# The second cross attention's chains: three batches five steps apart in place of two in step

## What is computed

```python
c_t = attn_mean @ V                                   # selection result, projected by Wv
x   = layernorm(x_text, g_norm_in, b_norm_in)         # x_text is layernorm(x) of the model
scale_in, shift_in = split(c_t @ W_film_in + b_film_in)
x   = x * (1 + mod_gate * scale_in) + mod_gate * shift_in
y   = s4d(x)                                          # a long convolution, by FFT, plus x * D_skip
scale_out, shift_out = split(c_t @ W_film_out + b_film_out)
y   = y * (1 + mod_gate * scale_out) + mod_gate * shift_out
xt  = x_text + y
h   = gelu(layernorm(xt, g_ffn, b_ffn) @ W1 + b1) @ W2 + b2
out = layernorm(xt + h, g_norm_out, b_norm_out)       # added to x
```

## Time and profile before

| what | value |
|---|---|
| median of 3 runs | 2420.95 us (2419.89 to 2425.65) |
| the profiled execution | 2421.84 us, of which the span is 2420.0 us |
| TensorE busy | 1858.7 us (77% of the span) |
| VectorE busy | 1291.5 us (53%) |
| ScalarE busy | 1060.2 us (44%) |
| GpSimd busy | 790.4 us (33%) |
| mean granted TensorE clock | 0.845 |

### The profile page before, as it was taken

The page is one execution under the profiler, slowest core; times in us unless marked ns, Lnnn a source line. Parts: engine busy times, 40 slices in busy tenths (PEclk is TensorE's granted clock), DMA queues, the critical chain, the costliest instruction groups (busy, mean ns, idle before and its releaser), DMA issues.

```text
span 2420.0 us, 34900 instructions
## 1 busy us (share of the span) xinstructions
PE 1858.7 (77%) x13676; PEld 1137.1 (47%) x13676; DVE 1291.5 (53%) x3082; ACT 1060.2 (44%) x1404; POOL 790.4 (33%) x686
## 2 busy tenths in 40 slices
PE   5789999999999988977466677876876477667752
PEld 2444544554454455655463244544544355455531
DVE  5143232323323016364884869979789754535557
ACT  1367567657657842212342435455455201005440
POOL 6144333335414100000320357857777021210001
PEclk7999999999999999996776556777867798888895
DMA  6645647556564400002000011212211330000000
GB/s 138 125 99 119 121 107 123 119 106 123 111 129 78 98 1 2 1 14 103 1 1 12 7 59 46 85 53 59 80 46 52 123 121 1 0 0 1 1 1 17
DMA packets 78046, 150.29 MB, mean 62 GB/s; under 512 B 15464, under 2 KB 63144, under 8 KB 71464
## 3 DMA queue, kind: packets, MB, share of 16 engines
q1 hardware_dynamic: 64304, 102.07, 14.9%
q0 software_dynamic: 12768, 42.59, 11.4%
q10 hardware_dynamic: 792, 3.17, 0.3%
HBM read 93.86 MB, written 2.62 MB: 40 GB/s over the span
## 4 chain that ended last, share of the span: by engine, by line
PE 48%; DVE 27%; ACT 12%; issue 7%; DMA 3%; POOL 3%; DVEq 0%; ACTq 0%; POOLq 0%; SPq 0%
PE R L112 29%; PE B L112 16%; ACT P L571 7%; DVE PM L1718 5%; DVE CA L1676 4%; ACT PM L1603 2%; PE B L178 2%; POOL KST L789 2%; DVE CA L1688 1%; DMA CT<-in_ctxT 1%; DVE T L1690 1%; ACT PS L2220 1%; DMA KST<-OV 1%; ACT RT L116 1%; DVE RT L604 1%
## 5 line engine op out<-in xcount | busy, mean ns | idle before, releaser
L571 ACT ACTIVATE P<-R 128x1024 f32<-128x1024 f32 x512 | 506.9, 1026 | 217.1 <-PE R L112 181.9
L112 PE MATMUL R<-QS,KST 100*128 100x256 bf16 x2048 | 295.8, 276 | 60.8 <-ACT P L571 53.8
L112 PEld LDWEIGHTS R<-QS,KST 100*128 100x128 bf16 x2048 | 169.4, 98 | 224.7 <-ACT P L571 121.8
L116 ACT ACTIVATE SC<-R 128x1024 f32<-128x1024 f32 x128 | 129.6, 1024 | 239.2 <-PE R L112 128.6
L200 POOL TENSOR_TENSOR LNrs<-LNve,pk_const 128x2 f32<-128x2 f32 x36 | 25.3, 703 | 605.1 <-DVE LNve L196 605.1
L1676 DVE MAX8 CA<-SC 128x8 f32<-128x128 f32 x1024 | 203.2, 277 | 15.8 <-ACT SC L116 14.8
L112 PE MATMUL R<-OV,QT 32*128 32x512 f32 x512 | 189.0, 826 | 0.0
L1791 POOL TENSOR_TENSOR ACC<-ACC,PM 128x4096 f32<-128x4096 f32 x21 | 186.2, 8866 | 1.7
L1718 DVE SCALAR_TENSOR_TENSOR PM<-SC,T,PM 128x4096 f32<-128x4096 f32 x32 | 149.6, 4711 | 39.1 <-ACT AT L116 20.6
L789 POOL DMA_DIRECT2D KST<-OV x300 | 145.1, 492 | 73.0 <-PE R L112 56.4
L112 PE MATMUL R<-P,VP 128*32 128x256 f32 x2304 | 154.8, 385 | 0.5 <-ACT P L571 0.3
(11 more groups left out here) (370 smaller groups left out, 3510.1 us busy)
## 6 DMA issues: line engine op xcount, KB each, us to landing
KST<-OV POOLq DMA_DIRECT2D x276, 128.0 KB, 10.8
CT<-in_ctxP SPq DMA_DIRECT2D x40, 768.0 KB, 4.6
CN<-in_ctxn SPq DMA_DIRECT2D x64, 384.0 KB, 3.3
CT<-in_ctxT SPq DMA_DIRECT2D x64, 192.0 KB, 2.4
KST<-OV SPq DMA_DIRECT2D x84, 128.0 KB, 10.2
KST<-in_ctxP ACTq DMA_DIRECT2D x4, 768.0 KB, 9.3
QS<-x_q POOLq DMA_DIRECT2D x24, 128.0 KB, 5.2
pk_a<-in_pk_a SPq DMA_DIRECT2D x1, 3014.0 KB, 17.6
```

Source lines behind the costliest of these rows:

```text
L112: return e.matmul(o, l, r, start=st, stop=sp, skip_group_check=True)
L116: return e.activation(o, i, ACT.Copy)
L571: e.activation(P[(32 * p + k0) % 3][:, :], ring.at(("s", p, k0))[:, :], ACT.Exp).then_inc(*EX.up((p, k0)))
```

## The change

The list is now `woven([14] * NB, lag=5, depth=3)`. Batch 0 starts alone in round 0, batch 1 joins in round 5, batch 2 in round 10, batch 3 in round 15. In a round with three chains, such as round 12, the list reads (0, 12), (1, 7), (2, 2). The last rounds, 24 to 28, hold batch 3 alone, in its steps 9 to 13. Most buffers exist three times (b % 3), HT and IT twice as before. ScalarE waits in s 8 until `h` of batch b - 2 is done, since IT and HT are shared with that batch, and in s 0 for the end of batch b - 3 instead of b - 2. The small layer norm tiles have four places instead of two. No operation is added or taken away.

```diff
-        LNst = sbt(ctx, "LNst", [128, 2, 2, 6])
+        LNst = sbt(ctx, "LNst", [128, 4, 2, 6])
...
-            for i in range(2):
+            for i in range(3):
...
-                    nb[nm, i] = sbt(c, f"{nm}{i}", sh)[:, :, :]
+                    if i < 2 or nm not in ("HT", "IT"):
+                        nb[nm, i] = sbt(c, f"{nm}{i}", sh)[:, :, :]
...
-            order = woven([14] * NB)
+            order = woven([14] * NB, lag=5, depth=3)
...
                 for b, s in order:
-                    i = b % 2
-                    u, CT2, CTT, YF, HN, HT, IT = (nb[nm, i] for nm in ("u", "CT2", "CTT", "YF", "HN", "HT", "IT"))
+                    i = b % 3
+                    u, CT2, CTT, YF, HN = (nb[nm, i] for nm in ("u", "CT2", "CTT", "YF", "HN"))
+                    HT, IT = nb["HT", b % 2], nb["IT", b % 2]
...
                     if s == 0:
-                        if b >= 2:
-                            e.wait_ge(*V.at(("x", b - 2)))
+                        if b >= 3:
+                            e.wait_ge(*V.at(("x", b - 3)))
...
                     elif s == 8:
+                        if b >= 2:
+                            e.wait_ge(*M.at(("h", b - 2)))
                         e.wait_ge(*M.at(("ht", b)))
```

More of the change, by code:

```diff
@@ L158, in build @@
         X = sbt(ctx, "X", [128, 2 * NB, 256])
-        LNst = sbt(ctx, "LNst", [128, 2, 2, 6])
-        LNmv = sbt(ctx, "LNmv", [128, 2, 2, 2])
-        LNve = sbt(ctx, "LNve", [128, 2, 2])
-        LNrs = sbt(ctx, "LNrs", [128, 2, 2])
+        LNst = sbt(ctx, "LNst", [128, 4, 2, 6])
+        LNmv = sbt(ctx, "LNmv", [128, 4, 2, 2])
+        LNve = sbt(ctx, "LNve", [128, 4, 2])
+        LNrs = sbt(ctx, "LNrs", [128, 4, 2])
         R = [ctx.enter_context(nc.psum_tensor(f"R{i}", [128, 1024], F32)) for i in range(3)]
@@ L1937, in scalar @@
                 for b, s in order:
-                    i = b % 2
-                    CT2, CTT, XF, HT, IT = (nb[nm, i] for nm in ("CT2", "CTT", "XF", "HT", "IT"))
+                    i = b % 3
+                    CT2, CTT, XF = (nb[nm, i] for nm in ("CT2", "CTT", "XF"))
+                    HT, IT = nb["HT", b % 2], nb["IT", b % 2]
                     if s == 0:
-                        if b >= 2:
-                            e.wait_ge(*V.at(("x", b - 2)))
+                        if b >= 3:
+                            e.wait_ge(*V.at(("x", b - 3)))
                         e.wait_ge(*M.at(("ct", b)))
```

## The result

The changed kernel takes 2455.53 us (median; 2452.06 to 2460.94), against 2421.5 (2419.89 to 2425.65) for the kernel before, run beside it: ratio 1.0131, 95% interval 1.0107 to 1.0155. Timed twice more it read 2449.56 and 2450.12, with ratios of 1.0092 (1.0062 to 1.0121) and 1.0106 (1.0084 to 1.0127). So it is slower by 23 to 34 us. (The ratios leave out two single executions that were far longer, one of e9 with 2534.91 us and one of e11 with 2987.48; the medians in the table further down include them.) The prediction said slower, but 2435.0 with a range of 2425 to 2443: the direction was right, the size was not, in any of the three.

A forecast was written before the change was run, and what follows sets the result against it. TensorE and VectorE take turns, neither full; in-order queues and TensorE's clock falls set the stage. 199.8 + 12.3 + 6.9 = 219.0 us against 204.85, +14.1, giving 2435.0 us, range 2425 to 2443.

The forecast's parts named there:

- The walk of the order: Stage's new order followed along the path that ends last, each piece at its traced duration, clock added afterwards: 199.8 us.
- Pieces with the clock high: Stage at full TensorE clock: 29.7 to y0, 34.2 to y1, 91.8 to y3, 44.1 to the end, sum 199.8 us.
- the last piece: Stage from y3 to its end, batch 3 finishing alone, clock high: 44.1 us.
- Sure falls: Five long TensorE idles in the stage ending at half speed, at xf0, y0, ht1, ht2, ht3: together 12.3 us.
- undecided 0 to 13.7: Stage restarts that may be slow, ht0, y1 to y3, xf1 to xf3: 0 to 13.7 us, half taken, 6.9.
- HAM oscillation: Skill's rule: short matmul bursts between waits pay for the clock's fall at each restart; every undecided restart lost, 2442 us.
- The rest costs nothing I can find: Loads, step 8's new wait, larger tiles and `stage_a1` behind the stage: no added cost found.
- 2.85 us idle leaves the clock high: Trace reading: the group after a 2.85 us TensorE idle took 3.72 us, not half speed; closer to 2428 us.
- The clock did not hold: Rival, chance 0.17: TensorE's clock never falls in the stage, or only early; at best stage 199.8, kernel 2416 us.
- The weave didn't overlap: Rival, chance 0.06: VectorE's idle time absorbs other batches' steps, period about 33 us, stage 26 us less, 2395 us.
- Worse: Rival, chance 0.06: VectorE's two-input operations meet GpSimd's more often; four more meetings and all slow restarts give 2446 us.

The follow-up runs named there:

- e9: Changed order, layer norm tiles local to the stage, plus matmuls nobody reads in TensorE's waits of the stage: 2437.84 us, ratio to before 1.0035, stage 204.0 us.
- e11: Weave with lag 3 for 5, local layer norm tiles, unread matmuls in the stage's TensorE waits: 2411.39 us, ratio to before 0.9934, stage 185.8 us.
- e10: Kernel before, with unread matmuls put into TensorE's waits of the stage: 2411.86 us, ratio to before 0.9946, stage 190.7 us.
- e14: Kernel before, with unread matmuls in TensorE's waits of the stage and in the part behind it: 2422.17 us, ratio 0.9987, stage 187.3 us.
- e15: Changed order with layer norm tiles local to the stage, second run of that kernel: 2446.73 us, ratio to before 1.0085, part behind 271.5 us.
- e16: The changed kernel itself, timed a third time, nothing altered: 2450.12 us, ratio to before 1.0106, stage 221.3 us.
- e2: Changed kernel with layer norm tiles back at two places and local ones for the stage: 2447.84 us, ratio to before 1.0103, part behind 280.1 us.

## Why the prediction missed

- **The walk of the order held.** Pieces with the clock high: 199.8 predicted; after less its slow instructions 201.0 (220.8 - 19.8), and 204.0 measured with the waits filled (e9), or 202.4 without the one slow `in`. Its intervals up to y3 were right to within 0.7 us each against e9; only the last piece was further off (44.1, measured 46.6, of which the slow `in` is 1.6). The mechanism was the one named: VectorE keeps to its queue, h0 stands ahead of batch 1's step 8, GpSimd's scaling stands ahead of X. That part was not luck.
- **The clock's size in the stage held, too.** Sure falls 12.3 predicted, 12.4 counted in after (xf0 1.7, y0 2.5, the three `ht` with what follows 3.0, 3.1 and 2.1). Of the undecided 0 to 13.7 I took 6.9; 7.5 came (fout1 1.8, y1 to y3 1.9 each, the later `xf` none). Stage: +14.1 predicted, +16.0 to +16.5 measured in three profiles of the changed kernel.
- **But it named the wrong culprit.** The argument put the loss on the clock's falls, and so did the rule that it took from the Trainium skill ("TensorE: Matmul & The Clock Gate", HAM oscillation). e9, e10 and e14 show that these cost the kernel before nearly as much (17.5 us of 204.8, against 18.6 of 221.0). What differs is the sum of pieces: 187.3 before, about 202.4 after. I had set 199.8 of the new order, free of the clock, against 204.85 of the old order with it. The sum is right that way, but it reads the order as a small gain with a penalty; it is a loss of about 15.
- **The step that failed:** "The rest costs nothing I can find", with "`stage_a1` behind it starts with a norm from a cold TensorE either way". It starts cold either way, but its first product took 5.83 us before and 6.11 or 6.12 after, and 92 us on there are restarts that come out at either clock with it. They came out slow in all three profiles of the changed kernel: a term set at 0 that measured +7.2 to +7.4. The earlier trace rows was read as "2.85 us idle leaves the clock high"; e15 and after show that 2.86 us end either way. Beside it the stage was 1.9 to 2.4 us over its term. The rest of the first comparison, 10.9 us ahead of the stage, is within what one kernel varies by. e16 shows the sum with little of that: -1.1 + 16.5 + 7.4 = 22.8 us over the profile of before, by the spans.
- **The range** let the undecided restarts of the stage vary but nothing outside it. Single profiles of one kernel differ by 12 us in where the stage begins. Had I put 0 to 7 us for the part behind and some 5 either way for the comparison itself, the range would have reached 2455 and held two of the three medians.
- **Rivals.** The clock did not hold (0.87 in the stage). The weave didn't overlap: 51 us from `y` to `y`, not 33. "Worse" came nearest in its size (2446) and was wrong in its mechanism: VectorE's two-input operations cost no more than before (103.66 us busy against 103.73).

Open: whether the old and the new order leave TensorE's clock as in these profiles every time, so that the +7 behind belongs to the change, or came more often by chance; why one kernel's last `in` takes 8.55 or 10.20 us; and what the tiles cost.

## What to carry to other kernels

Walk each in-order queue at the places where one batch waits for another: a lag is good or bad by what stands ahead of the critical step in the queues that it passes, and lag 3 for 5 was worth 17 us with the same operations. Compare sums of pieces only when both have the clock taken out, or both have it in, and give every later stage that restarts TensorE after 2 to 5 us of idling a term of its own. Matmuls that nobody reads, put into a wait of TensorE (behind no barrier and not ahead of the data that is due), bought back 14 to 18 us of a 205 us stage, more than any order tried here gained on the kernel before.

## What the hardware showed that was not expected

The same instruction after the same wait of 2.84 to 2.87 us took 3.72 us in some executions and about 6.7 in others, in one and the same kernel too (e15 and e2), and which of the two it was could be read off a product 90 us earlier (up to 5.83, or from 6.08 us on). A microsecond or two of delay at the end of one stage moved the next by 7 us, the wrong way as often as the right one. A fall can also follow short waits alone: in e9 the last `in` took 8.78 us, at a granted clock of 0.81, after idles of 1.63 and 0.79. And the work that nobody reads cost little: TensorE has 21% more busy time in e9's stage (177.6 us for 147.0) while the stage is 17 us shorter. The time it saved is in the instructions that follow it.
